# Expert gates spread by DMA instead of by TensorE in moe_3, context keys made pair by pair in attention_2, and unread products at two block seams

## The reference

```
# layer 2: attention of 16 heads of 64; keys and values from the tokens AND from 32 context rows
x = x + tanh(g_xattn[2]) * xattn2(ctx, layernorm(x))
# layer 3: 64 experts of width 64, top 6 out of 4 of 8 groups, gates normalised, plus a shared expert
x = x + tanh(g_ffn[3]) * ffn3(layernorm(x))
# in ffn3, with scores = sigmoid(x @ gate_w.T) and comb[token, expert] = the gate or 0:
y = sum over experts of comb[:, e] * (silu(x @ eg[e].T) * (x @ eu[e].T)) @ ed[e].T  + shared expert
```

## Time and profile before

| what | us |
|---|---|
| median of 3 runs | 2105.95 (2105.33 to 2106.55) |
| profiled execution, device time | 2109.82 |
| its span in the profile | 2108.0 |
| TensorE busy in it | 1930.4 (92%) |
| VectorE, ScalarE, GpSimd busy | 1260.1, 911.6, 818.9 |

### The profile page before, as it was taken

One profiled execution on the slowest core, in us unless ns is written; L12 is line 12 of the kernel. 1 busy time (PEld: TensorE's weight loads), 2 busy tenths in 40 slices (PEclk: granted clock), 3 DMA queues, 4 the chain that ended last, 5 costly groups with the idle time before them and its releaser, 6 DMA issues. The chain is left out here.

```text
span 2108.0 us, 32642 instructions
## 1 busy us (share of the span) xinstructions
PE 1930.4 (92%) x11413; PEld 1265.6 (60%) x11413; DVE 1260.1 (60%) x3293; ACT 911.6 (43%) x2134; POOL 818.9 (39%) x960
## 2 busy tenths in 40 slices
PE   5789899898999899998999989989898998989999
PEld 4466476555756567555765647656575675646655
DVE  6558576554866567464576647746375774654554
ACT  1154365364532456364542436627352662732221
POOL 3346266453520146463441107645252674620000
PEclk9799999999999999999999989999999999999999
DMA  5210000002030000002002000000200000030020
GB/s 204 92 37 1 1 1 2 1 1 81 1 127 1 6 1 2 1 1 81 1 26 102 1 5 1 1 1 2 81 1 1 1 2 0 2 120 1 22 104 5
DMA packets 33745, 59.10 MB, mean 28 GB/s; under 512 B 6448, under 2 KB 11184, under 8 KB 32944
## 3 DMA queue, kind: packets, MB, share of 16 engines
q1 hardware_dynamic: 33584, 57.03, 7.7%
HBM read 53.86 MB, written 3.16 MB: 27 GB/s over the span
## 5 line engine op out<-in xcount | busy, mean ns | idle before, releaser
L1288 POOL TENSOR_TENSOR rows<-rows,rinv 128x512 f32<-128x512 f32 x192 | 194.3, 1040 | 146.1 <-DVE rinv L1518 146.1
L2120 ACT ACTIVATE region_b<-psum 128x512 f32<-128x512 f32 x132 | 78.8, 597 | 258.7 <-PE psum L2065 258.5
L2161 DVE TENSOR_TENSOR region_b<-region_b,psum 128x512 f32<-128x512 f32 x128 | 87.8, 686 | 166.0 <-PE psum L2089 157.8
L1444 ACT ACTIVATE rows<-psum,nmax 128x512 f32<-128x512 f32 x192 | 130.1, 684 | 111.6 <-DVE nmax L1511 111.5
L2089 PEld LDWEIGHTS psum<-region_c,region_b 128*128 128x128 f32 x1024 | 133.7, 192 | 47.6 <-issue 27.9
L1510 DVE TENSOR_REDUCE lg<-psum 128x2 f32<-128x1024 f32 x128 | 155.5, 1215 | 3.4
L1522 DVE COPY turned<-psum 128x512 f32<-128x512 f32 x128 | 88.4, 691 | 94.4 <-PE psum L1350 94.1
L2064 PE MATMUL psum<-xnt,region_a 128*128 128x512 f32 x256 | 136.2, 614 | 5.9 <-DMA region_c<-in_weights 5.9
L1338 PE MATMUL psum<-region_a,region_b 64*128 64x256 f32 x1024 | 132.2, 397 | 7.1 <-DVE kctx L1497 4.2
L1007 ACT ACTIVATE region_b<-psum,b_t 128x512 f32<-128x512 f32 x128 | 87.4, 687 | 111.0 <-PE psum L1151 110.6
L2089 PE MATMUL psum<-region_c,region_b 128*128 128x128 f32 x1024 | 134.4, 275 | 0.7 <-DVE region_b L2164 0.7
(11 more groups left out here) (487 smaller groups left out, 4101.0 us busy)
## 6 DMA issues: line engine op xcount, KB each, us to landing
region_a<-w_centred SPq DMA_DIRECT2D x32, 258.0 KB, 5.3
region_a<-in_w SPq DMA_DIRECT2D x32, 256.0 KB, 4.5
region_a<-in_eg SPq DMA_DIRECT2D x32, 256.0 KB, 5.8
region_a<-in_eu SPq DMA_DIRECT2D x32, 256.0 KB, 5.8
region_c<-in_weights SPq DMA_DIRECT2D x32, 256.0 KB, 6.8
weights<-in_weights SPq DMA_DIRECT2D x1, 3489.0 KB, 15.8
w_centred<-region_a SPq DMA_DIRECT2D x8, 258.0 KB, 2.3
region_a<-in_w SPq DMA_DIRECT2D x1, 2048.0 KB, 12.2
```

Source lines behind the costliest of these rows:

```text
L1288: nc.gpsimd.tensor_tensor(row(u, j), row(u, j), rinv[:, 2 * u + j:2 * u + j + 1].broadcast_to([P, S]), ALU.mult).then_inc(s.pn, 1)
L1444: nc.scalar.activation(row(u, j), s_bank(u, j), ACT.Exp, bias=nmax[:, 2 * u + j:2 * u + j + 1], accum_out=sum_column(u // T, u % T, j)).th ...
```

## The change

In moe_3 the gates no longer go through bfloat16 parts and a product per item. `comb` is transposed in float32 (four products), ScalarE copies it to `gate_rows3` (64 x 512), SP stores that to DRAM (128 KB), waits until it is there, and loads for every item two rows back, each repeated on 64 partitions, into one of four tiles (two DMAs of 128 KB on the SBUF side; 64 in a block). VectorE waits for these, and does the multiplication by the gates two steps late for items 1 to 7 and one step late for items 8 to 15; `down` moves with it. `hn` has three buffers instead of two, and the wait for `down` moves from the first to the second multiplication. The first four chunks of experts are loaded ahead of `clear_set`, the other four between the gate loads; beside `front` its inputs come after chunk 0. At moe_3's end TensorE gets two unread products of 512 columns.

In attention_2 TensorE begins with five such unread products, and the context's key product of a pair follows that pair's key product.

```diff
-        select = part(region_b, 3072, [96, 1024]).bitcast(BF16).rearrange("p (e k) -> p e k", k=64)
-        gate3 = ...
+        hn = part(region_b, 1024, [P, 3, 512])
+        gate_rows3 = part(region_b, 3584, [E3, S])
+        spread3 = [pt[:, 0, :], pt[:, 1, :], part(ysb_flat, 0, [P, S]), part(ysb_flat, S, [P, S])]
+        gates3 = nc.dram_tensor("gates3", (E3, S), FP32, kind="Internal").ap()
...
                 def _(sp):
+                    if first_loads:
+                        first_loads(sp)
                     clear_set(sp, 1 - k % 2)
                     sync(sp)
...
                 def _(pe):
+                    keep_turning(5, bank(0))
                     transpose_tokens(pe, s, xn, bank(7))
...
-
-                    for c in range(PAIRS):
-                        mm = nc.tensor.matmul(bank(6)[:, K * c:K * (c + 1)], wkv2[:, P * c:P * (c + 1)], kvt[:, S:NK2],
-                                              start=True, stop=True)
+                        if kind == "k":
+                            mm = nc.tensor.matmul(bank(6)[:, K * c:K * (c + 1)], wkv2[:, P * c:P * (c + 1)], kvt[:, S:NK2],
+                                                  start=True, stop=True)
...
+        def spread_gates_3(sp, s):
+
+            landed = (s.spread0, s.spread1, s.spread2, s.spread3)
+            sp.wait_ge(s.rows, 1)
+            sp.dma_start(gates3[:, :], gate_rows3).then_inc(s.rows_out, 16)
+            sp.wait_ge(s.rows_out, 16)
+            for n in range(4 * CH3):
+                if n >= 4:
+                    sp.wait_ge(s.hc, n - 2)
+                for half in range(2):
+                    e = 2 * n + half
+                    sp.dma_start(spread3[n % 4][64 * half:64 * (half + 1), :],
+                                 gates3[e:e + 1, :].broadcast_to([64, S])).then_inc(landed[n % 4], 16)
+                if n % 4 == 1 and n // 4 < 4:
+                    load_experts_3(sp, s, (4 + n // 4,))
...
+            def gate_lag(i):
+                return 2 if 1 <= i < 8 else 1 if 8 <= i < 16 else 0
...
                 def turn_gates():
-                    pe.wait_ge(s.parts, 1)
...
+                    pe.wait_ge(s.comb, 1)
+                    for t in range(T):
+                        mm = nc.tensor.transpose(bank(4)[0:E3, P * t:P * (t + 1)], comb[:, t, :], ident[:, :])
                     mm.then_inc(s.gt, 1)
-                    pe.wait_ge(s.gts, 2)
-                    pe.wait_ge(s.select, 1)
...
-                    if 1 <= i < n_items and spread_banks == 2:
-                        spread(i)
-                    if i >= 2:
-                        down(i - 2)
...
+                    for n in down_at(i):
+                        down(n)
+                    if i == n_items + 1:
+                        keep_turning(2, bank(0))
...
+                        nc.scalar.activation(gate_rows3, bank(4)[0:E3, :], ACT.Copy).then_inc(s.rows, 1)
...
-                dve.wait_ge(s.comb, 1)
-                gate_parts(dve, link, s, comb[:, :, :].rearrange("p t (a e) -> p t a e", a=2),
...
+                def used_3(i):
                     dve.wait_ge(s.silu, i + 1)
...
+                        if i >= 4:
+                            dve.wait_ge(s.hc, i - 2)
+                        nc.vector.tensor_tensor(hn[:, i % 3, :], hsb[:, i % 2, :], bank(2 + i % 2), ALU.mult).then_inc(s.hu, 1)
+
+                def gated_3(i):
+                    n = i - 1
+                    dve.wait_ge(s.hu, i)
+                    dve.wait_ge((s.spread0, s.spread1, s.spread2, s.spread3)[n % 4], 32 * (n // 4 + 1))
+                    if i >= 2:
+                        dve.wait_ge(s.y, i - 1)
+                    nc.vector.tensor_tensor(htb[:, i % 2, :], hn[:, i % 3, :], spread3[n % 4], ALU.mult).then_inc(s.hc, 1)
...
             def gpsimd(pool):
-                nc.gpsimd.tensor_copy(select[:, :, :], over(fold_h[:, :], 2, [96, 32, 64])).then_inc(s.select, 1)
...
+            def first_loads(sp):
+                load_experts_3(sp, s3, (0,))
+                load_inputs(sp, sf, b_front)
+                load_experts_3(sp, s3, range(1, 4))
...
```

More of the change, by code:

```diff
@@ L255, in flamingo_kernel @@
         hsb = part(region_b, 0, [P, 2, 512])
[L256 to L257 removed]
+        hn = part(region_b, 1024, [P, 3, 512])
+        htb = part(region_b, 2560, [P, 2, 512])
+        gate_rows3 = part(region_b, 3584, [E3, S])
         hid = part(region_b, 0, [P, 2, FC * S])
@@ L580, in interleave, with block_of @@
                 due = next(side, None)
-        def block_of(k, sync, main, side=None, when=None):
+        def block_of(k, sync, main, side=None, when=None, first_loads=None):
             def program(eng, of_main, of_side):
@@ L2011, in back, with load_experts_3 @@
             return record(tensor=tensor, vector=vector, scalar=scalar, gpsimd=gpsimd)
-        MOE_3 = (*NORM, "logits", "sig", "comb", "select", "parts", "gt", "gts", "spread", "g", "silu", "hu", "hc", "y", "dve",
-                 "x", *LOADS)
-        def load_experts_3(sp, s):
+        MOE_3 = (*NORM, "logits", "sig", "comb", "gt", "rows", "rows_out", "spread0", "spread1", "spread2", "spread3", "g", "silu",
+                 "hu", "hc", "y", "dve", "x", *LOADS)
+        def load_experts_3(sp, s, chunks):
             loads = (s.load0, s.load1, s.load2, s.load3)
-            for c in range(CH3):
+            for c in chunks:
                 if c >= 4:
@@ L2030, in store, with moe_3 @@
             sp.dma_start(out[b:b + 1].rearrange("o (t p) d -> p (o t) d", p=P), xs[b % 3][:, :, :]).then_inc(stored, 16)
-        def moe_3(s, b, spread_banks=2):
+        def moe_3(s, b):
             x = xs[b % 3]
@@ L2040, in used, with gated_at, down_at @@
                 eng.wait_ge(s.hc, 1) if i == 0 else eng.wait_ge(s.hu, i)
-            def spread_bank(i):
-                return bank(4 + i % spread_banks)
+            def gate_lag(i):
+                return 2 if 1 <= i < 8 else 1 if 8 <= i < 16 else 0
+            def gated_at(step):
+                return [i for i in range(max(step - 2, 0), min(step + 1, n_items)) if i + gate_lag(i) == step]
+            def down_at(step):
+                return [i for i in range(max(step - 4, 0), min(step - 1, n_items)) if i + gate_lag(i) + 2 == step]
             def tensor(pe):
@@ L2067, in turn_gates @@
                 def turn_gates():
-                    pe.wait_ge(s.parts, 1)
[L2069 to L2073, removed]
-                    mm.then_inc(s.gt, 1)
-                    pe.wait_ge(s.gts, 2)
-                    pe.wait_ge(s.select, 1)
[L2078 to L2083, removed]
+                    pe.wait_ge(s.comb, 1)
+                    for t in range(T):
+                        mm = nc.tensor.transpose(bank(4)[0:E3, P * t:P * (t + 1)], comb[:, t, :], ident[:, :])
+                    mm.then_inc(s.gt, 1)
                 def down(i):
@@ L2160, in vector @@
                     else:
[L2161 to L2164, removed]
+                        if i >= 4:
[8 more added lines that the diff above has]
+                    nc.vector.tensor_tensor(htb[:, i % 2, :], hn[:, i % 3, :], spread3[n % 4], ALU.mult).then_inc(s.hc, 1)
+                for i in range(n_items):
+                    used_3(i)
+                    for n in gated_at(i):
+                        if n >= 1:
+                            gated_3(n)
                     yield i
@@ L2218, in sync @@
             def sync(sp):
-                load_experts_3(sp, s3)
+                spread_gates_3(sp, s3)
                 store(sp, s3, b)
-            block_of(k, sync, moe_3(s3, b, spread_banks=1), back(s2, b_back, bank(6), bank(5), set_f), lambda hop: hop)
+            block_of(k, sync, moe_3(s3, b), back(s2, b_back, bank(6), bank(5), set_f), lambda hop: hop,
+                     lambda sp: load_experts_3(sp, s3, range(4)))
         def moe_3_beside_front(b, b_front):
@@ L2226, in moe_3_beside_front @@
             sf = sems(k % 2, FRONT, s3)
+            def first_loads(sp):
+                load_experts_3(sp, s3, (0,))
+                load_inputs(sp, sf, b_front)
+                load_experts_3(sp, s3, range(1, 4))
             def sync(sp):
-                load_inputs(sp, sf, b_front)
-                load_experts_3(sp, s3)
+                spread_gates_3(sp, s3)
                 store(sp, s3, b)
-            block_of(k, sync, moe_3(s3, b), front(sf, b_front, bank(6)), lambda hop: hop)
+            block_of(k, sync, moe_3(s3, b), front(sf, b_front, bank(6)), lambda hop: hop, first_loads)
         def moe_3_alone(b):
@@ L2242, in sync @@
                     sp.wait_ge(stored, 16 * B)
-            block_of(k, sync, moe_3(s3, b))
+            block_of(k, sync, moe_3(s3, b), None, None, lambda sp: load_experts_3(sp, s3, range(4)))
         front_beside_setup(0)
```

10 lines of the change are left out of this document (removed).

## The result

The changed kernel takes **2083.43 us** (median of 4 runs, 2081.06 to 2085.98), the kernel before 2105.64 beside it: a ratio of 0.9892, 95% interval 0.988 to 0.9905. It is faster by 22.2 us, not by the 48.0 forecast, and outside the range of 2044 to 2079. The profiled execution took 2085.98 us, its span is 2084.2.

What follows compares the result with a forecast made beforehand. The prediction took TensorE, busy for 92% of the span, to bound the kernel. Its terms summed to -48.0 us, taking the median from 2105.95 to 2058.0 us, range 2044 to 2079.

Steps and rivals of the forecast that it cites:

- A: Items of moe_3: the spread product leaves TensorE, 0.22 us each, an item alone 2.83 to 2.61; -27.3 us.
- Rivals 1 and 2: Ring of gate tiles decides, slower, 2158, chance 0.04; gates' store and first load late at each head, 2089, chance 0.07.
- B: Heads of moe_3: `up` 2 starts earlier, 5.1 us beside front, 4.5 beside back, less half a possible clock loss; -17.9 us.
- F: Side functions beside moe_3: with shorter items a side hop can come late; between 0 and 8, +1.5 us.
- C: End of moe_3: two unread products lengthen three seams by 0.5 us each; +1.5 us.
- D: Head of attention_2: five unread products cost 3.2 us and save 10.0 by full clock in the 32 passes; -6.8 us.
- S: First 16 score passes in attention: half of the 3.2 us lost in batches 1 and 2 comes back; -1.6 us.
- E: Context keys beside the pairs in attention: scores start 0.65 us later in each of four blocks; +2.6 us.
- Number 4: TensorE waits for VectorE's side hops in three blocks, the spread product's gain kept only alone: +20.5, 2078, chance 0.10.

Runs made afterwards that it cites:

- the even lag: The changed kernel with moe_3's second multiplication two steps late for all items from 1 on: 2077.05 us, ratio 0.9855.
- that version: Changed kernel plus the even lag, front's tokens one item later, work behind them two, GpSimd's filling after them, two unread products in moe_3 alone: 2058.01 us.
- the one with the shift: The changed kernel with the even lag and the front's work in moe_3 from its third step two items later: 2065.85 us, again 2069.37.

## Why the prediction was wrong

- **A, the spread product, -27.3: right.** 0.22 an item in every stretch without a wait, and 2.61 an item alone. The DMA side held: store 2.2 us (forecast 2.3), gate loads 2.9 to 3.0 in the median and 6.2 at most, SP 0.6 an issue (forecast 0.45). Rivals 1 and 2 are refuted.
- **B, the heads, -17.9: right for two of four blocks.** Alone the block fell by 10.6 us (11.1 up to the issue of the last store) where A and B gave 11.3. Beside back it fell by 7.7 where they gave 10.6, and the even lag brought 2.6 more; the clock did fall after the 2.00 us of waiting alone (up 2 took 3.44 us for four passes), and not after as long a wait beside back, nor alone in the kernel with the even lag. Beside front the gain of 4.7 at `up` 2 came and was spent two items later.
- **F, the side functions, +1.5: this step failed.** I had put it between 0 and 8 us, from VectorE's share of busy time. But a share over 40 us says nothing about one chain: norm statistics, GpSimd's powers, four operations slowed to 2.58, transposes. That chain still stood behind the gates: its end came 1.6 us earlier, the user at its end 4.9. Taking its waits away, with the lag's, took the time from 2083.4 to 2058.0: the term was **+25** by the medians. By the table of blocks it was +21.7: 10.1 and 9.0 in the two blocks beside front, 2.6 beside back. Of the rest 0.9 is the block alone, where the clock now held, and 2.8 lie in no block of moe_3.
- **"VectorE's wait for `down` now comes one product later, which helps": wrong at the two falls of the lag.** I read the lag's steps in the diff and priced neither. Making it even was worth 6.4 us of that 25 by the medians, 9.2 by the blocks.
- **C, +1.5: right**, 0.36 x 3 = 1.1.
- **D, S and E, together -5.8: too large.** With C the part was to bring 4.3 and brought 1.3, or nothing on the kernel before. D's 10.0 and S's 3.2 were read from one execution in which the clock fell more often in attention_2 than in two others. E's delay came as told: the wait for `kctx` is 1.50 instead of 1.04, and the scores start 17.21 us after the first product (726.83 to 744.04), where 19.56 less the 2.97 of slow passes were 16.59 before: 0.6 later each, forecast 0.65.
- **The rivals.** Number 4, the side bounds the blocks, is the one that came, at +20.5 and a chance of 0.10, but not with its mechanism. It had the spread product's gain lost in each of three blocks; that gain stayed (0.22 an item), and what was lost were the gains of the heads and the waits at the lag's falls, almost all in the two blocks beside front. That its price lies near the 22 to 25 measured is luck. Its witness against it, was the average.

The sum with A and B as forecast, F and the attention part as measured: -27.3 - 17.9 + 25.4 - 1.3 = -21.1 us, against -22.2. As the 25.4 is itself a difference of measured times, this says no more than that A and B are there once the waits are gone. The blocks say it directly: in that version the four moe_3 blocks are 44.1 us shorter than before, where A, B and C gave 43.7. That its time comes to the forecast to the tenth is luck all the same: it lacks some 3 us of the attention part, and its five runs lie between 2053.8 and 2067.3.

## What to carry to other kernels

When a change makes the front of a block start earlier, follow the next few instructions that the busy engine meets, each back through its chain to an event that did not move, or moved less: the gain lasts until the first of them. Price that by the chain in the timeline, not by the engines' busy shares. And before charging a clock's fall to a place, profile the same kernel twice: a term read from falls that wander is worth their mean.

## What the runs showed of the hardware that was not expected

- Four VectorE operations of one source tile take 1.12 us together, and 2.58 beside two of GpSimd's products of 1.04 us each, in the same place of the same block. One by one they took 1.07, 1.08, 0.34 and 0.34 us: the first two ended 0.08 us after a product of GpSimd each, the others ran beside none. The Trainium skill, "SBUF — State Buffer", section on the two separate sides, says that VectorE in a two-port mode and GpSimd lock one pair of ports, whoever comes second being blocked for the whole instruction; the two timelines agree with it, though the mode that VectorE was in they do not show.
- An idle TensorE of 2.00 us was followed by half clock in moe_3 alone and not beside back, in the same execution; alone it was followed by full clock in the kernel with the even lag, by half clock again in the one with the shift.
- The times of a kernel spread with the granted clock: of 15 runs of the kernel before, measured together, those at 2101.5 us had a mean clock of 0.974 to 0.976, that at 2113.3 had 0.969.
- 131,072 bytes of gates to 64 partitions from one row of memory land in 2.9 us, 256 times over, and move 33 MB that the kernel did not read before, with no cost that any block shows.
